# Pacing the pointer scatters of a four-layer graph network's dense stage, and 48 in place of 56 early gathers

## The reference

```python
h = jnp.maximum(_layernorm(x, axis=-1), 0.0)
x = x + _L0_gnn_ref(h, node_type_4, src, dst, edge_type_8, ...)   # typed attention
h = jnp.maximum(_layernorm(x, axis=-1), 0.0)
x = x + _L1_gnn_ref(h, ..., src, dst)      # differences along edges, then relu(h_diff @ W + b)
h = jnp.maximum(_layernorm(x, axis=-1), 0.0)
x = x + _L2_gnn_ref(h, edge_index, ...)    # sum of neighbours, a two-layer perceptron
h = jnp.maximum(_layernorm(x, axis=-1), 0.0)
x = x + _L3_gnn_ref(h, ..., src, dst)      # attention with four heads, layer norm
```

## Time and profile before

| | us |
|---|---|
| timed runs (3) | 6629.22, 6645.62, 6647.14 |
| their median | 6645.62 |
| the profiled execution | 6621.41 |
| its span, first to last instruction | 6619.6 |
| PE busy | 4767.0 (72%) |
| DVE busy | 4454.2 (67%) |
| POOL busy | 3727.8 (56%) |
| ACT busy | 2385.6 (36%) |

### The profile page before, as it was taken

The page is one execution under the profiler, slowest core; times in us unless marked ns, Lnnn a source line. Parts: engine busy times, 40 slices in busy tenths (PEclk is TensorE's granted clock), DMA queues, the critical chain, the costliest instruction groups (busy, mean ns, idle before and its releaser), DMA issues. The chain is left out here.

```text
span 6619.6 us, 72686 instructions
## 1 busy us (share of the span) xinstructions
PE 4767.0 (72%) x18455; PEld 2642.0 (40%) x18455; DVE 4454.2 (67%) x7915; ACT 2385.6 (36%) x6652; POOL 3727.8 (56%) x3983
## 2 busy tenths in 40 slices
PE   0101477766799999789997888566587878778886
PEld 0100255544444455356664444222233334444443
DVE  5100488866788888699996666566567766666666
ACT  0100388756433333245553333122122333333333
POOL 1777300155466666200007887888777757777787
PEclk9655799988899999899995555555578877776666
DMA  9000133344333344299993332344455542222221
GB/s 353 21 7 14 56 117 118 116 122 125 85 84 84 84 85 88 52 264 286 285 268 84 83 83 75 98 112 112 95 145 148 150 112 64 64 64 65 64 60 41
DMA packets 845867, 733.47 MB, mean 111 GB/s; under 512 B 545388, under 2 KB 552514, under 8 KB 845328
## 3 DMA queue, kind: packets, MB, share of 16 engines
q1 hardware_dynamic: 543408, 519.54, 27.2%
q0 software_dynamic: 102464, 90.84, 7.5%
q10 hardware_dynamic: 199584, 118.45, 5.9%
HBM read 455.90 MB, written 276.55 MB: 111 GB/s over the span
## 5 line engine op out<-in xcount | busy, mean ns | idle before, releaser
L1366 POOL DMA_INDIRECT df_hs<-u,keep_idx x396 | 508.2, 1283 | 830.7 <-POOLq L243 710.3
L883 POOL DMA_INDIRECT sc_xg<-t,keep_gather x396 | 447.5, 1130 | 383.9 <-DVE sc_h L196 207.9
L805 POOL DMA_INDIRECT den_xd<-t,keep_gather x224 | 234.0, 1045 | 719.1 <-DMA xd<-den_xd 651.7
L1366 POOL DMA_INDIRECT hd_gat<-u,keep_idx x396 | 484.2, 1223 | 157.8 <-issue 117.4
L1899 POOL DMA_INDIRECT out_x<-hd_x,keep_scat_out x396 | 457.5, 1155 | 148.5 <-issue 119.9
L797 POOL DMA_INDIRECT t<-keep_ptr_pay,keep_scat_ptr x396 | 396.2, 1001 | 256.5 <-issue 131.9
L1366 POOL DMA_INDIRECT ml_gat<-u,keep_idx x396 | 401.8, 1015 | 157.7 <-issue 65.2
L1366 POOL DMA_INDIRECT pr_gat<-sd,keep_idxsd x396 | 413.5, 1044 | 104.3 <-issue 71.5
L220 DVE TENSOR_REDUCE den_dn_ss<-den_dn_sq 128x8 f32<-128x512 f32 x297 | 198.2, 668 | 328.9 <-issue 172.0
L754 PE MATMUL den_ps_dhid<-den_dh2t,keep_weights 64*128 64x512 f32 x396 | 129.5, 735 | 358.0 <-issue 323.9
L1355 PE MATMUL at_ps_m<-at_vx,keep_msg_twice 128*128 128x512 f32 x792 | 364.7, 604 | 23.2 <-DVE at_vx L1246 23.2
(11 more groups left out here) (314 smaller groups left out, 13003.4 us busy)
## 6 DMA issues: line engine op xcount, KB each, us to landing
u<-den_dh SPq DMA_DIRECT2D x198, 256.0 KB
t<-tab_row ACTq DMA_DIRECT2D x99, 272.0 KB, 11.3
tab_x<-in_x SPq DMA_DIRECT2D x99, 256.0 KB
den_dx<-in_x SPq DMA_DIRECT2D x99, 256.0 KB
out_x<-den_dx SPq DMA_DIRECT2D x99, 256.0 KB
sc_et<-in_etype_row SPq DMA_DIRECT2D x99, 256.0 KB
at_v<-vt SPq DMA_DIRECT2D x198, 128.0 KB
at_et<-in_etype_row SPq DMA_DIRECT2D x99, 256.0 KB
```

The lines of the kernel that those rows point to most:

```text
L805: pool.indirect_dma_start(xd[i][:, u, :], None, e.T0, bass.IndirectOffsetOnAxis(ap=e.gather0[:, b, TU + u:TU + u + 1], axis=0), bounds_che ...
L883: pool.indirect_dma_start(xg[i][:, u, :], None, e.T0, bass.IndirectOffsetOnAxis(ap=e.gather0[:, b.n, u:u + 1], axis=0), bounds_check=NP - ...
L1366: pool.indirect_dma_start(gat[i][:, u, :], None, table, bass.IndirectOffsetOnAxis(ap=idx_all[:, c:c + 1], axis=0), bounds_check=rows - 1, ...
```

## The change

In dense POOL now waits before every sixth scatter: ahead of scatter 6k it waits until DVE has incremented x2_done k times (k from 1 to 65). Nothing else in the order of POOL's queue changes. EARLY goes from 56 to 48, so LATE has 51 groups, dense gathers 192 times and not 224, and scores gathers destinations 204 times and not 172. Head goes from 66 to 71.

```diff
-EARLY = 56
+EARLY = 48
 LATE = [b for b in range(NG) if b * (NG - EARLY) // NG != (b + 1) * (NG - EARLY) // NG]
...
-        head = count * 66 // 99
+        head = count * 71 // 99
...
             def _(pool):
                 pairs = e.T0.rearrange("n (a b) -> (n a) b", b=2)
+                PACE = 6
                 for c in range(CH):
+                    if c % PACE == 0:
+                        wait(pool, den.x2_done, c // PACE, e.pool_passed)
                     pool.indirect_dma_start(pairs, bass.IndirectOffsetOnAxis(ap=e.scat_ptr[:, c:c + 1], axis=0),
                                             e.ptr_pay[:, c, :], None, bounds_check=NP * TW // 2 - 1,
                                             oob_is_err=False).then_inc(ptr_out, 16)
```

## The result

| | before | after |
|---|---|---|
| median | 6640.85 us (4 runs, 6629.22 to 6647.14) | 6161.26 us (4 runs, 6150.66 to 6170.69) |
| ratio | | 0.9279 (95%: 0.9255 to 0.9303) |
| the profiled execution | 6621.41 | 6153.16 |
| its span | 6619.6 | 6151.4 |

Faster by 480 us, where 470 were forecast. That holds for the conditions of this comparison. In later sets of runs the unchanged kernel before took not 6640 but 5887 to 5895 us, and there the same change was worth nothing (ratio 0.9998). Ratios compare fast runs alone; the one slow run, of the kernel with paced gathers when it ran a second time, took 8593.35 us at a granted clock of 0.62.

The account below looks back on a forecast made before the run. Long unbroken runs of POOL's indirect DMAs were taken to hold PE in dense. 891 + 31 + 4 + 18 + 85 = 1029 against 1503.7 us gains 475, less 5 in scores: 6151, plus 24 for the median: 6175 us, range 6105 to 6370.

Parts of the forecast that it names:

- 98 groups, POOL silent: Dense, group 0 to group 98: 9.09 us each, as where POOL is silent; 891 us.
- start: Dense's first chunks: one stall of 10 us set against 6 us for two short first groups; +4 us.
- scatter bursts: Dense, 66 groups with six scatters beside each: 9.56 us a group instead of 9.09; +31 us.
- run of 24 gathers: Dense, POOL's first 24 gathers, unbroken and following a chunk of scatters, delay PE; +18 us.
- the other 168 gathers: Dense's last 28 groups: the remaining gathers beside them cost 0.51 us each; +85 us.
- scores: Scores, eight more groups gathered there: PE stays the bound, POOL's idle time takes the gathers; +5 us, ends −15 and +42.
- to the median: Whole kernel: the timed runs' median lies 24 us above the profiled execution, so 6151 becomes 6175 us.
- First rival: Dense beside scatters: bursts run into the next, 12.16 us a group, +172 us, 6347 us; chance 20%.
- Second rival: Dense beside scatters: PE gets nothing during six scatters, then recovers; 19.3 us a group, +643, 6818 us; chance 7%.
- Third rival: Dense beside scatters: small writes hurt wherever they lie; 15.95 us a group, +422, 6597 us; chance 4%.
- The full queue: Dense beside scatters: if POOL's full queue of 8 instructions hurts, six never fill it; sum 31 us lower.
- SP at head 71: Dense, SP's first store at about 849 us: first gathers done at 837, so covered by about 10 us.

Follow-up runs that it names:

- the kernel with paced gathers: Kernel after with dense's gathers paced too (wait before every sixth DMA, head 70): 5897.25 us, ratio 1.0002; in a later set 5889.46 us, ratio 1.0003.
- the bursts of 24: Kernel after with scatters in bursts of 24, each released after four groups, instead of bursts of six: 6431.52 us (one run).
- the pace alone: Kernel before plus only the waits at every sixth scatter, EARLY 56 and head 66 kept: 6189.10 us, ratio 0.9328.
- the last profile: Kernel before, unchanged, profiled again in a later set of runs: 5896.73 us (one run).

## Why the prediction was right

It forecast 6175 us, range 6105 to 6370; 6161.26 was measured. The profiled execution was put at 6151 and took 6153.16. Term by term, for group 0 to group 98:

| term | forecast | measured | from |
|---|---|---|---|
| 98 groups, POOL silent | 891 | 891 (taken over) | five groups with four gathers beside them: 45.3 / 5 = 9.06 |
| start | +4 | +9 | four groups 45.1 − 36.4 |
| scatter bursts | +31 | +34 | 62 × (9.64 − 9.09) |
| run of 24 gathers | +18 | +15 | 23.8 − 9.1 |
| the other 168 gathers | +85 | +86 | 322.8 − 26 × 9.09 |
| from group 0 to group 98 | 1029 | 1034.5 | 1203.4 − 168.9 |
| scores | +5 | +2.2 | 1025.6 − 1023.4 |
| to the median | +24 | +8 | 6161.3 − 6153.2 |

The forecast gain was 470 us and 480 was measured; the mechanism held. Two of the terms that carry weight came from rows of the nearest case: 9.09 from the stretch where POOL is silent, 0.51 us a gather from the gathers of the kernel before.

The price of the bursts did not, and that 31 us came so near to 34 is in part luck. The prediction takes 9.56 us from seven groups with six to eight DMAs beside them, "since a burst of six with a pause is what they are". They are not. Six of the seven lie beside the first DMAs of something longer: the groups from 1289, 1405, 1493, 1530 and 1581 beside the heads of runs of 20, 16, 16, 16 and 20, and that from 1371 beside a run of 8 which another of 12 follows after 0.8 us. The loss of those runs falls into the group behind, which took 21.6, 17.7, 18.6, 17.7, 13.9 and 15.6 us. Only the group from 1433.5 (9.90) has a run of 9 with a pause on both sides, and the next took 8.93. Two groups of the same kind, from 1328.8 (9.41) and 1558.5 (9.25), were passed over. What the seven rows do show is that the first DMAs of a run cost little, and short bursts turned out to be little but such firsts. The mechanism was right; the row it was priced from was not the row it was called.

Only the start was off by more than its size. Late results now fall into group 2 (17.3 us) and group 3 (15.4), before the pace takes hold, beside a run of 24 scatters (167.0 to 198.1): one stall of 10 us was allowed for, and there were two. The term to the median was 16 us too high, which is the spread of single runs and not part of the mechanism. Where the prediction says that one PE instruction is let through for each scatter, it had only the two counts; the steps of 1.40 us above bear it out roughly.

**First rival, bursts cost as the gather stretch does (12.16).** Falls: 9.64. Its reason, bursts that run into one another, shows in small: a run of 15 scatters without a break, from 710.6 to 730.3, and beside it the longest group. Of the 62 groups of the paced stretch 42 take less than 9 us, 7 take 9.4 to 10.4, ten 10.9 to 11.4 and three 13.1 to 17.4.

**Second rival, every chunk shuts PE out (19.3).** Falls: the longest group of the paced stretch took 17.4.

**Third rival, the loss belongs to the scatters (15.95).** Falls under the hold, by the bursts of 24 and by the pace alone: the same scatters cost 2.8 or 22 us by how they are cut.

**The Trainium skill's rule**, page SBUF — State Buffer, section Who interferes with whom, that PE never waits on anyone. In the first profile the trace disagrees (ACT waited 60.75 us for PE's result); in the last profile of the same kernel it agrees (59 groups beside 395 scatters). The section speaks of SBUF ports, and whether the hold is one of ports no run shows. The prediction took the first for a property of kernel and chip. It was a condition that comes and goes.

**The full queue** (the Trainium skill, page Advanced Engine Details and Errata, section Engine Queue Depths): a sum without the 31 us for bursts was named for it. 34 were measured. Some 12 of them lie beside the run of 15 and one of 8 scatters (groups of 17.4 and 13.1 us), the rest beside runs of seven and fewer, which doesn't bear it out.

**SP at head 71.** POOL's last scatter ended at 800.5 (forecast: about 802), its first 24 gathers were through at about 834.5 (837). No wait of SP for gathers shows in the waits from 790 on. The cover held.

What the prediction left out is a case of its own: that the loss in the profile may be none of the kernel's. Nothing in the one profile of before could have told; three timed runs within 0.3% of each other looked like a constant. That case ends at ratio 1.000, and it had only a part of the 2% for "within 0.3%". That the comparison met the same condition as the profile was, in this sense, luck.

## What to carry to other kernels

Look for stretches where an engine that issues nothing to PE and shares no data with it, here POOL with indirect DMAs, coincides with PE's results coming tens of microseconds late; if that is what the trace shows, cut the row of DMAs into bursts of six with a wait for the consumer engine's own progress. The whole change cost nothing where it wasn't needed (ratio 0.9998). Where it was, it took 7.2% of the time, the pace alone 6.7%. And when a single loss of hundreds of microseconds has no cause in the program, profile the unchanged kernel again at another time before crediting the cure: most of the difference can be a condition of the machine.

## What the runs showed of the hardware

- Two conditions of the same program: 6632 to 6641 us with PE held under indirect DMAs of POOL, 5887 to 5895 without. The instructions of POOL are the same in both (1000 and 1003 ns a scatter, 0.30 us between two).
- Under the hold a row of indirect DMAs costs by its length: 22.1 us for a run of 24 scatters, 33.6 for one of 36 gathers, 112.0 us a group of dense in an unbroken row. By an estimate from four runs of 20 to 36 the first 7 to 13 are free.
- In the unbroken row PE's results come at 1.40 to 1.42 us an instruction, with a scatter every 1.28 us beside them.
- A break of 1.3 us and more (2.2 on average) instead of 0.30, once in six scatters, brings 112.0 us down to 9.64. With a pause of 3 us inside a run of 24, in which POOL waits for no other engine, the loss was 9.3 and 14.5 us instead of some 22. Limiting the DMAs in flight to four changes nothing (112.0).
- Under the hold even the paced kernel loses: 6161 us against 5886 without it. Of 621 us that dense loses to it (1503.7 − 882.6), the change won back 469.
